# Tokens in runs of four, two transfers for the experts' rows, and side work at other steps

## The reference

```
xn  = layernorm(x)
q, k, v = xn @ W_attn + b_attn, in 16 heads of 8 channels
s   = q k^T - mean;  s = s / mean(|s|) * gain;  causal
r   = max(s, 0)^4;   att = r / (sum(r) + 1e-6)
a   = (att v) @ W_proj + b_proj
f   = sum over the 2 best of 8 experts: weight * expert(xn)
expert(t) = silu((t w1 + b1) * (t w2 + b2) @ wg + bg) @ w3 + b3
out = x + a + f
```

## Time and profile before

| what | value |
|---|---|
| runs | 835.26, 840.07, 841.84 us (median 840.07) |
| the profiled execution | 838.95 us, its span 836.8 us |
| PE busy | 749.6 us of 5,839 records |
| DVE, ACT, POOL busy | 681.2, 677.0, 595.7 us |
| mean granted TensorE clock | 0.953 of full |

### The profile page before, as it was taken

How to read it: one execution, slowest core, us unless ns; L and a number is a source line. 1 busy time by engine, 2 the same in 40 slices (tenths; PEclk the granted TensorE clock), 3 DMA queues, 4 the chain that set the end, 5 groups by cost and what they waited for, 6 DMA issues and landing times.

```text
span 836.8 us, 17802 instructions
## 1 busy us (share of the span) xinstructions
PE 749.6 (90%) x5839; PEld 341.0 (41%) x5839; DVE 681.2 (81%) x1874; ACT 677.0 (81%) x1521; POOL 595.7 (71%) x534
## 2 busy tenths in 40 slices
PE   7878877778999899999999999999999898999877
PEld 6622121213444354444444445444444444443215
DVE  7669887879878988887888978788887977888882
ACT  4768878778988788898888888898888887889870
POOL 4017675855898778776977698588778768778890
PEclk9987887889999999999999999999999999999797
DMA  8883021154325324232533444044323432320394
GB/s 262 261 253 151 33 72 47 45 165 147 85 64 164 97 69 125 94 107 47 134 108 96 92 133 119 23 131 110 113 89 100 126 93 71 104 59 17 81 139 113
DMA packets 58348, 90.84 MB, mean 109 GB/s; under 512 B 8960, under 2 KB 41344, under 8 KB 58256
## 3 DMA queue, kind: packets, MB, share of 16 engines
q1 hardware_dynamic: 43200, 75.21, 32.0%
q0 software_dynamic: 10784, 12.53, 6.6%
q10 hardware_dynamic: 4272, 1.98, 0.8%
HBM read 61.29 MB, written 28.06 MB: 107 GB/s over the span
## 4 chain that ended last, share of the span: by engine, by line
PE 42%; DVE 21%; ACT 14%; POOL 11%; issue 11%; DMA 1%; DVEq 0%; ACTq 0%; SPq 0%; POOLq 0%
PE bank L967 17%; DVE W L1290 11%; PE bank L1002 7%; ACT U L826 6%; PE bank L982 5%; DVE junk_V L1282 4%; PE bank L1023 4%; POOL W L664 4%; PE bank L1031 3%; POOL W L675 3%; ACT W L842 3%; ACT junk_A L818 2%; PE bank L1007 2%; DVE W L1294 2%; PE bank L891 1%
## 5 line engine op out<-in xcount | busy, mean ns | idle before, releaser
L1290 DVE SCALAR_TENSOR_TENSOR W<-bank,U 128x512 f32<-128x512 f32 (+1 forms) x512 | 300.7, 648 | 28.5 <-ACT U L826 24.3
L967 PE MATMUL bank<-W,VS 128*10 128x512 f32 (+3 forms) x1536 | 302.1, 515 | 23.7 <-ACT W L842 14.5
L967 PE MATMUL bank<-U,usel 128*10 128x512 f32 (+3 forms) x1536 | 298.6, 513 | 0.0
L826 ACT ACTIVATE U<-bank 128x512 f32<-128x512 f32 (+1 forms) x512 | 252.0, 589 | 23.6 <-PE bank L1031 17.4
L1282 DVE TENSOR_SCALAR_CACHE_REDUCE junk_V<-bank 128x512 bf16<-128x512 f32 (+3 forms) x445 | 218.2, 533 | 64.0 <-PE bank L1023 57.6
L675 POOL TENSOR_TENSOR W<-W 128x1024 f32<-128x1024 f32 (+2 forms) x159 | 234.0, 1480 | 36.1 <-DVE W L1290 28.1
L664 POOL TENSOR_TENSOR W<-W,causal 128x512 f32<-128x512 f32 x127 | 164.3, 1294 | 98.2 <-DVE W L1290 72.5
L842 ACT ACTIVATE W<-W 128x256 f32<-128x256 f32 (+2 forms) x225 | 189.9, 869 | 22.4 <-POOL W L664 22.1
L1031 PE MATMUL bank<-QS,KS 48*128 48x512 bf16 (+3 forms) x768 | 153.0, 335 | 21.0 <-DVE W L1290 12.7
L818 ACT ACTIVATE junk_A<-bank 128x512 bf16<-128x512 f32 (+3 forms) x195 | 87.9, 460 | 46.0 <-PE bank L1023 45.0
L1023 PE MATMUL bank<-KS,QS 48*128 48x512 bf16 (+3 forms) x640 | 101.2, 325 | 2.3 <-DVE parts L1227 1.6
(11 more groups left out here) (162 smaller groups left out, 681.4 us busy)
## 6 DMA issues: line engine op xcount, KB each, us to landing
wb<-in_experts SPq DMA_DIRECT2D x39, 707.0 KB
qk_parts<-parts SPq DMA_DIRECT2D x8, 768.0 KB, 6.0
KS<-qk_parts SPq DMA_DIRECT2D x192, 32.0 KB
QS<-qk_parts SPq DMA_DIRECT2D x192, 32.0 KB
xt_all<-sorted_x SPq DMA_DIRECT2D x39, 130.0 KB, 5.8
sorted_x<-xt_all SPq DMA_DIRECT2D x3, 1300.0 KB, 12.2
xn_row<-weighted_y POOLq DMA_DIRECT2D x6, 512.0 KB, 7.3
v_stationary<-vb SPq DMA_DIRECT2D x4, 640.0 KB, 4.9
```

Source lines behind the costliest of these rows:

```text
L826: act.activation(U[n % NU][:, g, 0:w], score(n, g), ACT.Relu).then_inc(u_ready, 1)
L967: last = pe.matmul(acc[32 * g:32 * g + VW, lo:HALF], usel[:, :] if of_u else VS[q % 2][:, j, :, g], (U if of_u else W)[n % NU][:, g, 0:HAL ...
L1290: vec.scalar_tensor_tensor(W[n % NU][:, g, 0:w], score(n, g), 0.0, U[n % NU][:, g, 0:w], ALU.max, ALU.mult).then_inc(w_done, 1)
```

## The change

1. **Layout.** A partition now holds runs of four neighbouring tokens: in each half batch of 512 tokens, partition p has tokens 4p to 4p+3. xr is packed without gaps (128 words a token), so x, the experts' rows and the result move in contiguous pieces of 2 KB and not of 512 bytes. PE gets the tokens in that order by reading yT with a stride of four columns (`in_half`).
2. **Experts' rows.** Two accumulating DMAs of 2 MB each, for all four batches, at the steps FFN_TO + 2 = ALL - 10 and FFN_TO + 6 = ALL - 6. The second waits until the first has landed. `gat` and its PE matmuls are gone; DVE's last additions wait for both transfers.
3. **Giving back.** A table `BACK_AT` puts rows_of_pair and the give-backs into steps that have room for them (ROOM: two in the positions 4, 5, 6 and 8, one in 0 and 7, none elsewhere).
4. **Side work.** FFN_TO is two steps later; S_SUMS, S_TURN, S_SCALE and S_MOVE are one later, S_TIMES and S_PROJ two.
5. **The end.** ACT stores batches 0 to 2 in one DMA, which waits for the last sums and rows to be in (so that it runs behind their loads). PE runs further dummy matmuls (`keep_busy`) behind the sums and between the steps of the scales.

```diff
-    FFN_FROM, FFN_TO = SCATTERS // PER_STEP + 3, ALL - 14
+    FFN_FROM, FFN_TO = SCATTERS // PER_STEP + 3, ALL - 12
...
+    ROWS, BACK_AT, due = -1, [[] for _ in range(ALL)], []
+    ROOM = [1, 0, 0, 0, 2, 2, 2, 1, 2, 0, 0, 0]
+    for n in range(ALL):
+        due += [(p, m) for kind, p in FFN_AT[n - 1] if n and kind == "my" for m in [ROWS, *range(2 * len(tiles_of(p)))]]
+        while due and len(BACK_AT[n]) < (ROOM[n % NS] if n < FFN_TO - 2 else 2):
+            BACK_AT[n].append(due.pop(0))
...
-    S_SUMS, S_TURN, S_SCALE, S_MOVE, S_TIMES, S_PROJ = 3, 5, 5, 9, 14, 16
+    S_SUMS, S_TURN, S_SCALE, S_MOVE, S_TIMES, S_PROJ = 4, 6, 6, 10, 16, 18
...
-    ADD_AT = [ALL - 8 + i for i in range(TOPK * NE)]
+    ADD_AT = [FFN_TO + 2, FFN_TO + 6]
...
-        xr = xn
+        xr = xn_row[:, :, :].rearrange("p t c -> p (t c)")[:, 0:NT * C].rearrange("p (t c) -> p t c", c=C)
...
+        by_half = lambda v: v.rearrange("b (h p t) c -> p (b h) t c", h=CH, p=P)
+        xr_h = xr.rearrange("p (h t) c -> p h t c", t=TB // CH)
+        y_h = ys_d[0:TOPK * N].rearrange("(k h p t) c -> p k h t c", k=TOPK, p=P, t=TB // CH)
+        in_half = lambda c, t: yT[:, c * HALF + t:(c + 1) * HALF:TB // CH]
...
-                    sp.dma_start(xr[:, :, :], x_v).then_inc(x_again, 16)
+                    sp.dma_start(xr_h, by_half(x)).then_inc(x_again, 16)
...
+            def experts_in(k):
+                if k == 0:
                     for par in range(2):
                         pool.wait_ge(fy[par], 32 * sum(len(tiles_of(p)) for p in range(par, NPAIR, 2)))
...
+                pool.wait_ge(res_y, CH * NE)
+                pool.wait_ge(res_x, B)
+                wait(pool, res_e, 16 * k)
+                pool.dma_start(xr_h, y_h[:, k], accum_op=ALU.add).then_inc(res_e, 16)
...
+                for p, m in BACK_AT[n]:
+                    if m == ROWS:
+                        rows_of_pair(p)
+                    else:
+                        give_back(p, m)
...
-            for b in range(NE):
-                act.wait_ge(res_e[b], 16 * TOPK)
-                act.dma_start(out_v[:, b * TB:(b + 1) * TB, :], xr[:, b * TB:(b + 1) * TB, :]).then_inc(res_out, 16)
+            act.wait_ge(res_e, 16 * TOPK)
+            act.wait_ge(sums_in, 16 * (2 * NE + 2 + 4))
+            act.wait_ge(y_in[NE], 16 * 9)
+            act.dma_start(by_half(out)[:, 0:CH * NE], xr_h[:, 0:CH * NE]).then_inc(res_out, 16)
...
-            pe.wait_ge(gathered, 16 * TOPK)
...
+            keep_busy(8)
+            pe.wait_ge(sums_in, 16 * (2 * NE + 2 + 4))
+            keep_busy(2)
+            for k in range(1, NSC):
+                pe.wait_ge(fin_v, NSC * NE + k)
+                keep_busy(1)
...
             for c in range(CH):
                 vec.wait_ge(proj, CH * NE + c + 1)
+                vec.wait_ge(res_e, 16 * TOPK)
```

More of the change, by code:

```diff
@@ L276, in layer_kernel @@
         x_again, res_x, res_y = sem("x_in_again"), sem("x_and_bias"), sem("attention_added")
-        res_e = [sem(f"experts_added{b}") for b in range(NE)]
-        gathered, mask_v = sem("gathered"), sem("w_masked_vec")
+        res_e, mask_v = sem("experts_added"), sem("w_masked_vec")
         res_out = sem("result_out")
@@ L523, in _ @@
                                  ).then_inc(sc_in, 16)
-                if n == FFN_TO + 4:
-                    for k in range(2):
-                        sp.wait_ge(fy[k], 32 * sum(len(tiles_of(p)) for p in range(k, NPAIR, 2)))
-                    for k in range(TOPK):
-                        sp.dma_start(gat[:, k, :, :], y_v[:, k, NE * TB:, :]).then_inc(gathered, 16)
             for par in range(2):
@@ L1080, in _ @@
                 pe.wait_ge(yn_ready, NE + c + 1)
-                for n in range(c * TB // CH, (c + 1) * TB // CH):
-                    last = pe.matmul(flat[2][:, n * C:(n + 1) * C], yT[:, n * P:(n + 1) * P], wp[:, :],
-                                     start=False, stop=True, skip_group_check=True)
+                for t in range(TB // CH):
+                    last = pe.matmul(bank[2][:, c, t * C:(t + 1) * C], in_half(c, t), wp[:, :], start=True, stop=True)
                 last.then_inc(proj, 1)
```

41 lines of the change are left out of this document (9 added, 32 removed).

## The result

| | before | after |
|---|---|---|
| median of 4 runs | 837.66 us (834.01 to 841.84) | 860.69 us (859.63 to 862.16) |
| ratio, 95% interval | | 1.0275 [1.0216, 1.0333] |
| profiled execution, its span | 838.95, 836.8 us | 859.63, 857.9 us |
| PE, DVE, ACT, POOL busy | 749.6, 681.2, 677.0, 595.7 us | 768.3, 687.4, 677.3, 588.8 us |

The change makes the kernel 2.75% slower, 23 us; the forecast was 828.4 us, faster by 1%, and its range ended at 838.5.

What follows compares the result with a forecast made beforehand. PE was taken as the bound from 187 to 772 us, then POOL, then a serial tail. Gains of 4.0 + 0.8 + 2.8 + 2.8 + 1.3 = 11.7 us gave 827.3, or 828.4 as median; range 820 to 838.5.

Steps and rivals of the forecast that it cites:

- Multiplication by the scales and give-backs in other steps: Long stretch: 78 give-backs leave the masked steps, so PE waits less for POOL; gain 4.0 us (0 to 6.3).
- The three waits: PE's weight load waited three times for POOL's multiplication by the scales, 4.6 us in all; these were to go.
- PE's 94%: From 187 to 772 us PE is busy 550.4 of 585 us; taken to make PE the bound there.
- Rival C: Steps without a mask, positions 4 to 7: POOL becomes the bound, PE waits for late squares; 850 us, chance 0.08.
- FFN_TO two steps later: Two steps' worth of experts' PE work, 2.6 us, leaves the full stretch; gain 0.8 us (0 to 2.6).
- The stretch with 17% idle: Where PE has idle time, and where the 2.6 us of experts' work was to move.
- the two rows quoted: The records of w1/w2 and of wg, 77 us each, read as some 1.3 us of PE work a step.
- The strided yT as weights: PE loading its projection weights from yT with a stride; taken to cost nothing.
- spreading and projection together: Tail: dummy matmuls raise PE's clock during the spreading of the scales and the projection; gain 1.3 us (0 to 3.2).
- Two accumulating transfers: From 786 to 817 us: two DMAs replace six, POOL stands some 2 us; gain 2.8 us (4.3 to a loss of 2).
- The piece: An accumulated piece of 2 KB was to occupy a DMA engine for 190 ns (128 to 260).
- The stores and the last sums: Tail: with the stores moved behind them the last sums take 2.1 us, not 4.91; gain 2.8 us (2.4 to 3.4).

Runs made afterwards that it cites:

- c1: The kernel before with only the giving back moved (the table BACK_AT alone); ratio 1.0072.
- b3: The kernel before with only the side work's new steps (S_SUMS to S_PROJ of the change); ratio 1.0016.
- e1: c1 with the scales of batches 0 to 2 worked out with one operand in PSUM, the first five operations in one step; ratio 1.0014.
- e2: The whole change with the scales of batches 0 to 2 worked out with one operand in PSUM, the first five operations in one step; ratio 1.0119.
- b1: The kernel before with only FFN_TO two steps later (ALL - 12), so the experts' turns fall on 145 steps; ratio 1.0084.
- b2: The kernel before with all the experts' turns shifted two steps later, still on 143 steps; ratio 1.0315.
- d1: a4 with the scaled product written to a new tile in PE's reading order, transfers at ALL - 13 and ALL - 8, multiplication at 16, projection at 20; ratio 0.9884.
- b4: a4 with the second accumulating transfer at ALL - 4 in place of ALL - 6; ratio 1.0028.
- a4: The change with FFN_TO, side work and giving back as before; layout, two transfers and new end stay; ratio 1.0025.

## Why the prediction was wrong

*Multiplication by the scales and give-backs in other steps: forecast a gain of 4.0, bounds 0 to 6.3.* The three waits did go. The failed step is the lower bound: "Nothing goes if another wait takes their place; a gain elsewhere is excluded by PE's 94%". A loss elsewhere was never priced. Alone the giving back costs 0.72% (c1) and the side work gains nothing (b3). What took the place of the waits is a hold that I had no term for: the new order sets POOL's squares, row weighting and give-backs one behind another at positions 5 to 9 of a quad, where DVE works out the scales from two operands in SBUF. e1 and e2 show it by taking the holds away, with the limit said there. The upper bound was too high as well: 4.6 us is what the weight loads waited, and PE's matmuls waited for only 3.2 us of it, twice, in the kernel before:

```profile
PE bank L1046 <- POOL yT L624: 3.2, 2, 2.1
```

Rival C had the place right (positions 4 to 7 of a quad, POOL) and the victim wrong: it let PE wait for late squares in all quads; in fact DVE was shut out, in the quads that have side work. Its time, 850 us, was nearer than the forecast, at a chance of 0.08.

*FFN_TO two steps later: forecast a gain of 0.8, bounds 0 to 2.6.* It costs 0.84% alone (b1), 7 us. Two readings were wrong. The stretch with 17% idle begins at 786 us, and step 178, now the last with a turn, is over before 773 us in the trace of before, so the work never moved there; and the two rows quoted, 77 us each, make 1.1 us a step and not 1.3. But the step that failed is the bound of 0: I counted the work that leaves the stretch and not the rhythm in which the turns meet the quads: the steps without a turn had lain at positions 4, 9 and 10 and now fall on all twelve. In b2 and b1 PE runs short in such steps, its clock falls, and the next 3.4 us cost double. The earlier trace rows had shown that, once; I used it as a cost that would go and not as a warning of what a new shortage would cost.

*The strided yT as weights, at nothing.* 0.33 us a load against 0.19: 1.8 us of the projection in the tail (3.97 against d1's 2.16), and in the long stretch up to 6.6 us in the loads, with 5.3 us more of busy time in the matmuls behind them. The tail hit its forecast by luck, by small errors that cancel: spreading and projection together gained 0.8 us (1.7 less 1.0) where 1.3 was taken, the sums 3.0 where 2.8 was.

*Two accumulating transfers: forecast a gain of 2.8, bounds 4.3 to -2.* The piece was right, 193 ns against 190. The wait was 4.3 us against 2, and the last steps lost 3.7 us: a term that was mis-sized, beyond its own end. Some 1.5 us of the 3.7 need not be the transfers', as b3, c1 and e1 lose as much there with the old ones. With the second transfer later the last steps take 5.1 us less (b4 against a4), so its place is what costs, and b4's tail takes 4.2 us more, so moving it alone wins nothing.

*The stores and the last sums*: 1.89 us against 2.1 forecast. Right.

**The sum of the loss.** Held operations 13 us (e2), turns 7 us (b1), everything but the three tables 2.1 us (a4, 0.25%): 22 of 23 us. That this comes so near is partly luck. The figures come from different pairs of kernels, the 13 us take out holds that the kernel before had too, and the three parts, alone 1.7% and together 2.5%, don't simply add up. Shown is that without holds the change loses 1.2%, and that without its three tables it loses 0.25%. Still open is why a step without a turn starves PE at positions 0 and 6 and not at 10, why the gaps at position 4 (0.72 us) made the clock fall only once, and how fast the kernel before is with its scales in PSUM; no kernel was made for these.

## What to carry to other kernels

When an edit moves work on one engine, look at what the others run beside its new place, and above all for DVE operations with both inputs in SBUF beside POOL's multiplications: a duration far above its row's minimum is a wait that no view of waits lists. An even spread of turns over a periodic schedule is itself a setting: changing its length by two steps moved its gaps to other positions and cost 7 us, and shifting it by two cost 3%. A busy share of 94% excludes no loss, since held and half-clock time count as busy; bound a "free" move below zero.

## What was not expected of the hardware

- A DVE operation of 128x1 with two inputs in SBUF took 4.36 us beside POOL's multiplications, as long as one of 128x128 (4.19, 4.34); with one input in PSUM 0.30.
- A weight load of 128x128 in float32 takes 192 ns with neighbouring columns and 329 ns with a step of four (16 bytes), at full clock.
- POOL's multiplication of 128x1024 takes 2.36 us in order and 4.16 us when it reads with that step.
- An accumulated piece of 2 KB takes 193 ns, a stored one of 2 KB at the end 0.534 x 8 x 16 / 784 = 87 ns (queue at 850:858 us, below); the ratio of 2.2 is near the 2.4 of pieces of 512 bytes.

```profile
q10 hardware_dynamic: 784, 1.57, 53.4%
```
